# State-space block of a four-block image kernel: ln(1+e) in one ScalarE instruction, its rounding compensation on VectorE and GpSimd in SBUF

## The reference, cut to what matters

```python
x  = _gn(x)                                   # group norm
xs, z = split(x @ W_in)
xs = silu(depthwise_conv4(xs) + conv_b)
dt, Bm, Cm = split(xs @ W_xproj)
dt = softplus(dt @ W_dt + b_dt)               # log(1 + exp(v))
deltaA  = exp(dt[..., None] * A)              # two states
deltaBx = dt[..., None] * Bm * xs[..., None]
h[t] = deltaA[t] * h[t-1] + deltaBx[t];  ys[t] = sum_n h[t] * C[t]
y = (ys + xs * D_param) * silu(z)
x = x + layernorm(y @ W_out)
```

## Time and profile before

| | |
|---|---|
| median of 3 runs | 698.72 us (695.61 to 700.11) |
| profiled execution, first to last instruction | 697.9 us |
| PE busy | 625.1 us (90%) |
| DVE busy | 535.1 us (77%) |
| ACT busy | 429.5 us (62%) |
| POOL busy | 385.2 us (55%) |
| state-space scan | from about 58 us to 196 us of the span |

### The profile page before, as it was taken

One profiled execution on the slowest core, in us unless ns is written; L12 is line 12 of the kernel. 1 busy time (PEld: TensorE's weight loads), 2 busy tenths in 40 slices (PEclk: granted clock), 3 DMA queues, 4 the chain that ended last, 5 costly groups with the idle time before them and its releaser, 6 DMA issues.

```text
span 697.9 us, 8622 instructions
## 1 busy us (share of the span) xinstructions
PE 625.1 (90%) x2812; PEld 275.6 (39%) x2812; DVE 535.1 (77%) x857; ACT 429.5 (62%) x737; POOL 385.2 (55%) x243
## 2 busy tenths in 40 slices
PE   3795888888789989999989999999999999986996
PEld 1232332233353332234434444343444444335982
DVE  6996899999934465888858787887878888685547
ACT  2478689899644331235555765748476565787772
POOL 2454788887512140216939779595968979430000
PEclk9997999999999997999989999999999999998999
DMA  9000000000015482404003040300304020200006
GB/s 328 7 0 0 1 0 0 0 0 0 1 45 140 112 199 54 106 1 91 0 1 90 1 91 0 71 21 9 83 0 91 0 31 1 30 1 0 1 1 241
DMA packets 28533, 32.36 MB, mean 46 GB/s; under 512 B 16976, under 2 KB 17104, under 8 KB 28368
## 3 DMA queue, kind: packets, MB, share of 16 engines
q1 hardware_dynamic: 27056, 27.33, 15.3%
q10 hardware_dynamic: 1440, 4.55, 2.7%
HBM read 5.83 MB, written 4.19 MB: 14 GB/s over the span
## 4 chain that ended last, share of the span: by engine, by line
PE 58%; DVE 19%; issue 8%; ACT 7%; POOL 4%; DMA 1%; SPq 1%; DVEq 0%; POOLq 0%; ACTq 0%
PE PS L1723 15%; PE PS L1710 10%; PE PS L1688 9%; PE PS L1599 5%; DVE RB L476 3%; PE PS L1608 2%; PE PS L1677 2%; PE PS L1743 2%; DVE RB L552 2%; DVE PS L544 2%; DVE RB L851 2%; DVE RB L559 1%; PE PS L1850 1%; DVE SM L456 1%; DVE SM L692 1%
## 5 line engine op out<-in xcount | busy, mean ns | idle before, releaser
L692 DVE TENSOR_REDUCE SM<-PS 128x1 f32<-128x512 f32 x256 | 165.0, 683 | 65.3 <-PE PS L1688 64.7
L1154 ACT ACTIVATE RB<-PS 128x512 f32<-128x512 f32 x256 | 138.9, 594 | 88.0 <-PE PS L1710 86.9
L1391 POOL TENSOR_TENSOR RB<-RB 128x1024 f32<-128x1024 f32 x60 | 141.1, 2372 | 7.1 <-DVE RB L721 4.8
L1710 PE MATMUL PS<-R 98*128 98x512 f32 x256 | 95.5, 452 | 1.3 <-ACT RB L1154 1.3
L1688 PE MATMUL PS<-R 96*128 96x512 f32 x256 | 88.7, 418 | 6.9 <-DMA R<-R 3.2
L1723 PE MATMUL PS<-RB 128*64 128x512 f32 x320 | 85.4, 616 | 0.0
L1710 PEld LDWEIGHTS PS<-R 98*128 98x128 f32 x256 | 38.8, 189 | 83.4 <-ACT RB L1154 53.9
L1526 PE MATMUL PS<-RA,W 128*128 (+1 forms) x128 | 63.1, 636 | 8.7 <-DVE RB L552 5.3
L1688 PEld LDWEIGHTS PS<-R 96*128 96x128 f32 x256 | 48.7, 193 | 43.1 <-DVE SM L692 18.9
L1391 POOL TENSOR_TENSOR EX<-EX,RB 128x1024 f32<-128x1024 f32 x24 | 56.5, 2373 | 0.8
L1723 PE MATMUL PS<-RB,RA 128*64 128x512 f32 x192 | 52.7, 627 | 0.0
(11 more groups left out here) (186 smaller groups left out, 1111.7 us busy)
## 6 DMA issues: line engine op xcount, KB each, us to landing
R<-WS SPq DMA_DIRECT2D x72, 128.0 KB, 2.4
X<-x SPq DMA_DIRECT2D x8, 512.0 KB, 7.4
RB<-RB SPq DMA_DIRECT2D x32, 128.0 KB, 4.0
RB<-RB ACTq DMA_DIRECT2D x14, 280.5 KB, 4.1
out<-X SPq DMA_DIRECT2D x7, 512.0 KB, 2.7
R<-R SPq DMA_DIRECT2D x20, 128.0 KB, 2.4
W<-pack SPq DMA_DIRECT2D x1, 1072.0 KB, 11.6
R<-R ACTq DMA_DIRECT2D x4, 128.0 KB, 3.3
```

What stands on the lines that cost most here:

```text
L692: v.tensor_reduce(MX[:, par, tile, h:h + 1], bank(2 + h), AX.X, ALU.max)\
L1154: act(slot[:, h * HALF:(h + 1) * HALF], bank(4 + h), ACT.Exp).then_inc(s["p_ready"], 1)
L1391: i = g.tensor_tensor(out, out, PT[j % SLOTS][par], ALU.add)
L1710: mm(bank(4 + h), stack(b, par, 1)[0:98, j * P:(j + 1) * P], stack(b, par, 0)[0:98, h * HALF:(h + 1) * HALF]).then_inc(s["t_mm"], 1)
```

## The change

What it does, part by part:

- ACT no longer writes u = 1 + e. The logarithm is taken of e with a bias of one in the same instruction, from SBUF (tE) and no longer from PSUM bank 0. It waits for e_done in place of nd_done.
- DVE's instruction computes w = (e + 1) - 1 from tE into a new tile tW (in WS), with one input and two immediate numbers. It waits for e_done in place of u_done, and for dt_done of two halves ago (tW's last reader).
- POOL has four instructions in place of three for each half: ln - w, then + e, then + relu, then times xs. It waits for nd_done (DVE) as well as ln_done.

```diff
+        tW = [WS[:, 0, h * HALF:(h + 1) * HALF].bitcast(F32) for h in range(2)]
...
             def soft(p, h):
                 n = 2 * p + h
-                v.wait_ge(s["u_done"], n + 1)
-                v.scalar_tensor_tensor(tE[h], bank(0), -1.0, tE[h], ALU.add, ALU.subtract)\
-                    .then_inc(s["nd_done"], 1)
+                v.wait_ge(s["e_done"], n + 1)
+                need(v, s["dt_done"], n - 1)
+                v.tensor_scalar(tW[h], tE[h], 1.0, 1.0, ALU.add, ALU.subtract).then_inc(s["nd_done"], 1)
...
                 act(tE[h], tE[h], ACT.Exp, scale=-1.0).then_inc(s["e_done"], 1)
-                a.wait_ge(s["e_done"], n + 1)
-                need(a, s["nd_done"], n)
-                need(a, s["ln_done"], n)
-                act(bank(0), tE[h], ACT.Identity, bias=ONE).then_inc(s["u_done"], 1)
...
             def soft_log(p, h):
                 n = 2 * p + h
-                a.wait_ge(s["nd_done"], n + 1)
+                a.wait_ge(s["e_done"], n + 1)
                 need(a, s["b_read"], n - 1)
-                act(tU[h], bank(0), ACT.Ln).then_inc(s["ln_done"], 1)
+                act(tU[h], tE[h], ACT.Ln, bias=ONE).then_inc(s["ln_done"], 1)
...
             def soft(p, h):
                 n = 2 * p + h
                 g.wait_ge(s["ln_done"], n + 1)
+                g.wait_ge(s["nd_done"], n + 1)
+                link(g.tensor_tensor(tU[h], tU[h], tW[h], ALU.subtract))
+                link(g.tensor_tensor(tU[h], tU[h], tE[h], ALU.add))
                 g.wait_ge(s["dt_read"], n + 1)
-                link(g.tensor_tensor(tM[h], tM[h], tU[h], ALU.add))
-                g.tensor_tensor(tM[h], tM[h], tE[h], ALU.subtract).then_inc(s["dt_done"], 1)
+                g.tensor_tensor(tM[h], tM[h], tU[h], ALU.add).then_inc(s["dt_done"], 1)
                 g.wait_ge(s["dt_done"], n + 1)
                 g.tensor_tensor(tU[h], tM[h], half(XS, p, h), ALU.mult).then_inc(s["dtx_done"], 1)
...
-                ch.enter(p - 2, 4)
+                ch.enter(p - 2, 6)
```

More of the change, by code:

```diff
@@ L297, in build @@
             g_ready xb_done xz_mm tap_done taps_done silux_done siluz_done
-            dt_mm b_mm c_mm o_mm v_mm e_done dta_read u_done dt_read nd_done ln_done dt_done dtx_done
+            dt_mm b_mm c_mm o_mm v_mm e_done dta_read dt_read nd_done ln_done dt_done dtx_done
             b_read da_done scan_done c_read hc_done y_done y_last sq_done r_done normed0 blk0_done sums_done
```

## The result

The changed kernel is slower: 706.88 us median of 4 runs (704.70 to 708.01) against 697.74 us for the kernel before beside it (695.61 to 700.11). The ratio is 1.0116, interval 1.0077 to 1.0156. So it costs about 9 us, and "slower by over 1%" is what both medians say, though each interval reaches down to 0.8%. A ratio on record is not the plain quotient of two medians and differs from it by up to 0.3%.

What follows compares the result with a forecast made beforehand. DVE bounds the scan at 7.94 us a half turn; POOL's list of 8.11 plus 0.56 for meetings, taken as 8.7, adds +10.6 us, with start and end +9.6: 708.3, said as 708.5 us, range 702 to 716.

Steps and rivals of the forecast that it cites:

- the sum: Whole scan: +0.2 first output instruction, +10.6 for fourteen half turns, -0.9 and -0.3 at the end; total +9.6 us.
- DVE sets the pace before; one ACT instruction less is worth nothing: Scan: DVE paces at 7.94 us a half turn; dropping L956 starts POOL 1.45 us earlier, 1.36 given back; value 0.
- DVE's new instruction, 0.41 us: DVE in the scan: 0.41 us against 0.68; 0.27 us less work a half turn, 3.8 us if DVE stayed the pace.
- POOL's list, 8.11 us: POOL in the scan: 6.69 us plus 1.42 for the added instruction is 8.11 a half turn, so POOL becomes the pace.
- The meeting term, 0.56 us: Scan half turn: L564 and the new DVE instruction delay POOL's next one by 0.56 us, giving 8.67, taken as 8.7.
- E: End of the POOL instruction L564 waits for; L564 and the new DVE instruction then finish at E + 0.94 us.
- the second rival: Scan: new DVE instruction loses its place behind L564 and slips into a gap; 8.35 to 8.45 us, about 704.8; chance 0.18.
- POOL loses the rest less 0.20: Where POOL waits for a running DVE instruction, it loses that instruction's remaining time less 0.20 us.
- DVE waits until POOL's end plus its own time less 0.14: Where DVE waits for a POOL instruction, it ends at POOL's end plus its own duration less 0.14 us.
- The whole-length rival: Scan: meetings cost whole lengths, or DVE is blocked twice; 9.1 to 9.4 us a half turn, 714 to 718; chance 0.15.
- Bounds: Meeting of DVE and POOL: at least nothing, 8.11 us a half turn, no gain; at most 9.4 us, DVE pacing again.
- Signs named ahead: Changed profile: 8.7 us pace, POOL without idle before output, long L565 and L538 or 1.8 us POOL instruction, DVE idle before L545.

Runs made afterwards that it cites:

- e8: The kernel before with only the ACT part changed: the logarithm reads e directly with a bias of one; 697.12 us, ratio 0.9964.
- e1: The changed kernel without POOL's added instruction, so w is left out; 691.99 us, ratio 0.9885, 7.65 us a half turn.
- e3: The changed kernel with both DVE instructions reading one operand from a PSUM bank of ones, result not the reference; 700.09 us, ratio 1.0023.
- e7: The changed kernel with w computed by two ACT instructions and no such DVE instruction; 713.64 us, ratio 1.0202.
- e5: The changed kernel with only L565 (the skip) reading a PSUM bank of ones for xs, result not the reference; 700.59 us, ratio 1.0041.
- e2: The kernel before plus one POOL instruction per half turn writing an unused tile, additions in the changed order; 711.40 us, ratio 1.0160.
- e4: The changed kernel with only the new DVE instruction reading its subtracted 1 from a PSUM bank of ones; 705.93 us, ratio 1.0062.
- e11: The changed kernel run once more, nothing altered; 708.46 us, ratio 1.0121, 8.59 us a half turn.

## Why the prediction was right, point by point

Predicted were 708.5 us and 8.7 us a half turn; measured were 706.88 and 708.46 us and 8.60. The marker is at +10.1 us where the sum said +9.6; without the 1.0 us that arose ahead of the scan it is +9.1, which is also the difference of the first pair of medians (9.14; the later pair has 8.54).

- **DVE sets the pace before; one ACT instruction less is worth nothing.** Right. In the changed kernel POOL starts its scan work 1.62 us after ACT's first e starts (58.99 to 60.61), before it was 3.05 us (58.00 to 61.05): 1.43 us gained, predicted 1.45. And it is given back: from e to the first L545 it is 7.01 us, before 7.04. That the scan as a whole began 0.99 us later (e at 58.99 instead of 58.00) happened ahead of any changed instruction; the table load ahead of it is 0.99 later too. e8 shows when the part has a value, namely if POOL gets no added instruction.
- **DVE's new instruction, 0.41 us.** Right: 413 ns at its shortest, 0.42 us in e1. e1 gives the gain that the prediction named for a DVE that stays the pace: 0.29 us a half turn, predicted 0.27.
- **POOL's list, 8.11 us.** Right within 0.06: e3 shows 8.05. Instruction starts are 1.34 and 1.35 us apart behind L1318 and L1319 and 1.47 behind L1321, so the added one costs 1.34, the lower of the two values that I had weighed, and not 1.42.
- **The meeting term, 0.56 us.** Right in size, 8.60 - 8.05 = 0.55, and **wrong in its path**, the order in which the engines get their turn. The prediction had L565 wait for E, the end of the instruction ahead, with the new instruction right behind it, so that POOL's next one loses E + 0.94 - 0.18 - 0.20. Instead L565 came 0.04 us behind or 0.14 ahead of E and took its bare 0.75 us (in every half turn from 78 to 182 us but the one at 95 us), took 0.29 to 0.48 us from L1323, and the new instruction lost its place to L1323. That is the order of the second rival. But the rival's price for it was too low: it let the new instruction slip into a gap for nothing, and took 0.23 us for L565. In fact L565 costs 0.38 on average and the late L538 0.18. Two errors of the rival, +0.15 and +0.18 us, bring its 8.11 + 0.23 = 8.34 to 8.67, and with a list of 8.05 to the measured 8.6. The right total is thus part luck: the forecast's path would have held only if two ready DVE instructions kept POOL out, which the earlier trace rows show for the two L762 and which does not hold here. Its own had the order that came, with L1391 between L428 and L429. What decides is open. The order of asking does not tell the cases apart: L538 was ready 0.35 us after L1323 had begun to wait and lost its place, but the second L762 too began 0.40 us after L1358 (at 214.39, against 213.99) and kept it.
- **POOL loses the rest less 0.20.** Close: less 0.13 to 0.14 here, in three instances (0.43 for 0.29, 0.61 for 0.48, and in e7 0.66 for 0.52). **DVE waits until POOL's end plus its own time less 0.14**: 0.12 and 0.13 (changed kernel, e5); e2 has 0.55 for an instruction of 0.75, less 0.20.
- **The whole-length rival** (9.1 to 9.4 us, 714 to 718 us) is out, and with it the price that I had drawn from the Trainium skill (SBUF — State Buffer, Who interferes with whom: whoever issues first gets the pair of SBUF ports that the two engines share, for the whole instruction, and the other "fully blocks"). In the trace the late one does wait for the end (L538 ends 0.29 us behind L1323), so the rule's order of events agrees. The price by whole lengths was my own step, and the page does not state it: one that waits loses only the rest of the other, and the two meetings make 0.55 us a half turn against the 1.0 of whole lengths. The nearest approach to it is e2, with 0.66 and 0.75 for one meeting.
- **Bounds.** "A gain is excluded, below nothing" held. The upper bound of 9.4 was never approached; 8.79 (e2) was the highest pace of all.
- **Signs named ahead.** POOL's instruction of 1.8 us: 1.75 in every second half. L538 above 0.41: 1.50. No idle time in front of L1329: right. POOL busy 28.21 of 30 us is 8.1 of 8.6. "DVE idle in front of L545 with POOL as releaser" was wrong: it happens once, at the start, for 1.2 us. DVE is filled to the brim, by its own 7.55 us and L538's wait of 1.09 us, together 8.64. That neither engine has a gap is, as I read it, why the lock holds: from L1323's end at 123.31 POOL reaches the end of the next L1321 at 130.10, and DVE reaches L565 at 130.14.
- **Sum.** First output instruction: 1.03 us later, of it 0.04 beyond the 0.99 from ahead of the scan, predicted +0.2. Half turns: +9.2, predicted +10.6, the difference being 14 x 0.1. The end: -0.2, predicted -0.9 and -0.3. This is the term that was mis-sized: I let the last L545 come right behind POOL's last `soft`, but in DVE's list L571 and L576 stand ahead of it, and L571 waited 0.48 us for ACT. L545 started 0.95 us behind the last L1329, 1.15 before.
- **What I had no bound for** was the form of e2 and e4, where L565 comes just behind POOL's start. It lay inside the range (8.79 us would have been +11 us), but the prediction's time line had only "in the middle of an instruction, or as the next starts" and priced both alike.

## What to carry to other kernels

When an added instruction fills the last idle time of an engine, ask who had been using that idle time. Here the instruction itself cost 0.11 us a half turn and the lost room for DVE's two-input instruction 0.55. Work out both engines' lists to a tenth of a microsecond and lay them over each other: an operand taken from PSUM instead of SBUF on the DVE side removed a meeting altogether (e3, e5), but check that the changed length doesn't move the other meeting to the dear side (e4). And take a shorter instruction for a gain only with e1's question answered, whether the work that it hands to the next engine has room there.

## What the runs showed that I had not expected

- DVE's L565 that asked 0.05 to 0.07 us after a POOL instruction had started took 1.75 to 1.77 us, and POOL then waited 0.71 us for it: 0.75 us lost in every second half turn of e2 and e4, and 0.66 to 0.67 in the others, where it asked 0.18 us after the start. The same instruction asking 0.3 us before POOL's start (changed kernel, 121.43 against 121.75) took 0.75 and cost POOL 0.29. So less than 0.4 us in arrival changes the cost of one meeting from 0.3 to 0.75 us. Most of that is no jump: ahead of POOL's start the cost grows with the part of L565 that is left, 0.29 us when it asks 0.32 ahead, 0.48 at 0.14 and 0.56 at 0.05 (e11); where the order turns round, 0.04 to 0.05 us ahead, it goes from 0.56 to 0.67.
- It follows that a DVE instruction 0.26 us longer *and without a meeting of its own* made the kernel's pace slower, 8.60 to 8.73 us (e4), although DVE alone was not the bound.
- The busy share hides this. DVE shows 28.74 of 30 us in the changed kernel, of which 1.09 us in each half turn is L538 standing still.
